# Transformer block on one core: another order inside the attention steps, and four row buffers for the routed tiles

## What is computed

```python
x = x + attention(layernorm(x))          # 16 heads of 32
#   q, k = layernorm(rope(x @ w_q)), layernorm(rope(x @ w_k))   per head
#   a = tril((q @ k.T) ** 4);  out = (a / a.sum(-1)) @ v;  out @ w_out
x = x + moe(layernorm(x))
#   logits = x @ gate.T; scores = sigmoid(logits); 4 of 16 experts chosen, by groups
#   each expert: (silu(x @ g.T) * (x @ u.T)) @ d.T, weighted and added;
#   one shared expert for every token
```

## Time and profile before

| | us |
|---|---|
| three timed runs | 1215.68, 1217.14, 1225.99 (median 1217.14) |
| the profiled execution | 1209.58, its span 1207.6 |
| PE, DVE, ACT, POOL busy | 958.4, 756.9, 563.6, 529.1 |
| the four batches of attention | 118.0, 149.4, 139.7, 112.0 |
| end of attention to the first scatter | 134.5 |
| first to last scatter of the routed tiles | 457.4 |

### The profile page before, as it was taken

How to read it: one execution, slowest core, us unless ns; L and a number is a source line. 1 busy time by engine, 2 the same in 40 slices (tenths; PEclk the granted TensorE clock), 3 DMA queues, 4 the chain that set the end, 5 groups by cost and what they waited for, 6 DMA issues and landing times. The chain is left out here.

```text
span 1207.6 us, 21002 instructions
## 1 busy us (share of the span) xinstructions
PE 958.4 (79%) x5770; PEld 455.7 (38%) x5771; DVE 756.9 (63%) x1663; ACT 563.6 (47%) x1009; POOL 529.1 (44%) x738
## 2 busy tenths in 40 slices
PE   5967789869777785984777799888888798878883
PEld 2432333324333332341343454444344344434441
DVE  2857865867888588849648665554455544545552
ACT  2347874866537665577235234333333233333330
POOL 0005663544415545367302003555555555555553
PEclk9988999888879887976868899899999989999996
DMA  8002333433323333655346896777777777778874
GB/s 330 13 35 93 118 105 137 140 119 112 107 88 100 137 107 110 236 204 192 107 148 207 304 319 184 193 185 184 174 188 191 178 179 181 190 174 193 183 187 78
DMA packets 76648, 193.48 MB, mean 160 GB/s; under 512 B 9904, under 2 KB 11056, under 8 KB 75312
## 3 DMA queue, kind: packets, MB, share of 16 engines
q1 hardware_dynamic: 58672, 149.53, 35.9%
q0 software_dynamic: 17920, 43.26, 19.6%
HBM read 131.67 MB, written 61.10 MB: 160 GB/s over the span
## 5 line engine op out<-in xcount | busy, mean ns | idle before, releaser
L743 PE MATMUL bank<-arena,xgT 128*128 (+1 forms) x1152 | 288.0, 387 | 3.6 <-ACT xgT L1029 3.1
L1065 POOL TENSOR_TENSOR s_p<-s_p,c_causal 128x128 f32<-128x128 f32 x256 | 153.8, 624 | 304.3 <-DVE s_p L1420 282.7
L485 PE MATMUL bank<-arena 128*128 128x512 f32 x384 | 196.5, 663 | 43.8 <-ACT arena L856 14.6
L1022 ACT ACTIVATE hT<-bank 128x512 f16<-128x512 f16 x96 | 57.3, 597 | 273.1 <-PE bank L753 273.1
L743 PEld LDWEIGHTS bank<-arena,xgT 128*128 128x128 f16 x1152 | 109.2, 100 | 133.1 <-issue 45.4
L1073 POOL TENSOR_TENSOR arena<-arena 128x768 f16<-128x768 f32 x68 | 113.0, 1662 | 87.8 <-ACT arena L821 87.7
L1109 POOL DMA_INDIRECT out<-yy,sidx x80 | 128.6, 1608 | 46.1 <-issue 44.6
L764 PE MATMUL bank<-wd,hT 128*128 128x512 f16 x576 | 146.0, 391 | 0.7 <-ACT hT L1022 0.7
L910 ACT ACTIVATE arena<-bank 128x512 f32<-128x512 f32 (+3 forms) x256 | 100.8, 439 | 93.2 <-PE bank L533 92.6
L1694 DVE TENSOR_SCALAR yy<-bank,hsc 128x512 f32<-128x512 f32 x80 | 60.0, 750 | 122.8 <-DMA out<-yy,sidx 116.6
L1029 ACT ACTIVATE xgT<-bank 128x1024 f16<-128x1024 f16 x96 | 98.2, 1023 | 78.7 <-PE bank L734 77.4
(11 more groups left out here) (172 smaller groups left out, 1390.2 us busy)
## 6 DMA issues: line engine op xcount, KB each, us to landing
wd<-w_scratch SPq DMA_DIRECT2D x82, 512.0 KB, 4.2
arena<-w_experts SPq DMA_DIRECT2D x34, 768.0 KB, 6.0
w_scratch<-arena SPq DMA_DIRECT2D x34, 768.0 KB, 4.5
arena<-w_scratch SPq DMA_DIRECT2D x17, 1024.0 KB, 7.7
xin<-x SPq DMA_DIRECT2D x4, 1024.0 KB, 5.5
arena<-x SPq DMA_DIRECT2D x4, 1024.0 KB, 4.8
x_scratch<-arena SPq DMA_DIRECT2D x4, 1024.0 KB, 5.2
xg<-xn_scratch SPq DMA_DIRECT2D x16, 256.0 KB, 4.5
```

The lines of the kernel that those rows point to most:

```text
L485: mm = pe.matmul(bk[:], xnT[:, c, m * P:m * P + P], wqkv[:, c, w * E:w * E + E], start=(c == 0), stop=(c == EC - 1))
L743: mm = pe.matmul(bank[2 + k][:], xgT[:, k, xh * EC + c, :], w, start=(c == 0 and xh + wh == 0), stop=(c == EC - 1 and xh == 1))
L1065: pool.tensor_tensor(d, d, C["causal"][:], ALU.mult).then_inc(p4_masked, 1)
```

## The change

It has two parts.

**In the attention steps** pieces are put in another order. PE runs `values` of a group's last block ahead of the v product instead of behind it, and in the last batch the logits are spread over steps 5 and 6. ACT does both halves of `qkT` ahead of the first square (the second half stood behind the second square), `copy_v` of blocks 1 to 3 moves from the head of step `4 m + 1` to the end of step `4 m`, `head_squares` moves to the end of step `4 m`. Most other entries of ACT's table move from the head of a step to the end of the step before, which is the same place. DVE's `finish` moves from the head of step `4 m + 1` to step `4 m`, right behind its `fourths`, and `choice_places` goes ahead of `centre`; in the last batch some of the routing goes one step later. SP's store of the normed rows goes one weight half earlier.

**In the routed tiles** the gathered rows have four buffers instead of two, POOL issues the gather of tile `t + 2` where it issued that of `t`, gather and scatter numbers have a semaphore each, and the loops of PE and POOL take four tiles in a turn; ACT, DVE and SP keep two.

```diff
 class Tile:
+    def turns(self, bufs, d=0):
+        n = self.n // bufs
+        c = self.lo // bufs + 1 + d
+        return c if self.r is None else (self.r if n == 1 else self.r * n) + c
...
+def tile_pairs(eng, lo, hi, step, n=2):
+    with eng.Fori(0, (hi - lo) // n) as r:
+        for j in range(n):
+            step(Tile(r, lo + j, n))
...
# SP
-                halves_of(b, 0, 2)
+                halves_of(b, 0, 1)
                 if b:
                     sp.wait_ge(xn16_ready, b)
                     sp.dma_start(xn_dram[N * (b - 1):N * b, 0:E]...
-                halves_of(b, 2, 4)
+                halves_of(b, 1, 4)
...
# PE
-                elif i == 5:
-                    for m in range(MB):
+                elif i in (5, 6):
+                    pe.wait_ge(x2T_sb, upto(pb, 3))
+                    for m in (2 * i - 10, 2 * i - 9):
                         logits(pb, m, bkA)
...
                     scores(b, i)
+                    if i and i % MB == 0:
+                        values(b, i - 1)
                     if b + 1 < B:
                         fill(b, i)
-                    if i:
+                    if i % MB:
                         values(b, i - 1)
...
-                    pe.wait_ge(xg_in[k], t.plus(-TB).uses() * 16)
+                    pe.wait_ge(xg_in[k4], t.plus(-TB).turns(4) * 16)
...
# ACT, sequence
                     square(b, i, 1)
-                    if nb < B and p == 0:
-                        if m:
-                            qkT(nb, m - 1, bkA, bkB, (1,))
-                        head_squares(nb, m)
                     square(b, i, 2)
                     fourth(b, i, 1)
                     square(b, i, 3)
                     fourth(b, i, 3)
+                    if nb < B and p == 0:
+                        if m:
+                            copy_v(nb, m, bkA)
+                        head_squares(nb, m)
...
                     split_next(b, i)
+                    if nb < B:
+                        behind(b, i)
...
# DVE
-                if p == 1 and m:
-                    finish(b, m - 1)
-                elif p == 2 and (m < MB - 1 or lb < B):
+                if p == 2 and (m < MB - 1 or lb < B):
...
                 if p == 0:
                     if m:
+                        finish(b, m - 1)
                         split_qk(nb, m - 1)
                     head_variance(nb, m)
...
+                if i == 15 and b:
+                    choice_places(pb, bkA)
+                if p == 3 and (m < MB - 1 or lb < B):
                     centre(nb if m < MB - 1 else lb, (m + 1) % MB)
...
# POOL
             def weight_and_rows(t):
                 weight(t.plus(-2))
                 pool.wait_ge(weights_here, t.at(-1 - TB))
-                pool.wait_ge(numbers, t.at(-1 - TB) * 2 if not t.below(TB + 4) else t.at(2 - TB))
-                if t.is_(NT - 1):
-                    gather_numbers(t.plus(-1), again=True)
-                else:
-                    gather_numbers(t.plus(1))
-                gather(t)
+                if t.r is not None or t.lo < NT - 3:
+                    pool.wait_ge(gather_no, t.at(3 - TB))
+                    gather_numbers(t.plus(3))
+                    gather(t.plus(2))
+                elif t.is_(NT - 3):
+                    pool.wait_ge(gather_no, RT)
+                    gather(t.plus(2))
+
+            def add_rows(t):
+                pool.wait_ge(y_sb, t.at(-3))
+                if not t.below(TB + 5):
+                    pool.wait_ge(added, t.at(-4 - TB) * 16)
+                pool.wait_ge(scatter_no, t.at(-3 - TB))
+                scatter_numbers(t.plus(-3))
+                scatter(t.plus(-4))
```

159 lines of the change are left out of this document (75 added, 84 removed).

## The result

The changed kernel takes 1228.59 us (median of 15 runs, 1219.36 to 1246.18) against 1217.14 us of the kernel before. The ratio is 1.008, with an interval of 1.005 to 1.011; a second measurement gave 1.012 (1.008 to 1.016). The ratio leaves out the slow runs, four of the 15 that were over 1.5% above the fastest; the median of the other eleven is 1226.7 us. So the kernel is slower by about 1%, and the forecast of 1192 us had the wrong sign. The time lies inside the stated range of 1160 to 1240, in the part that belongs to the first rival.

What follows compares the result with a forecast made beforehand. The prediction took the routed stage as a chain of scatters and attention as bound by badly timed meetings of in-order streams. Gains of 20 us in attention and 5 in routed tiles gave 1217.1 - 25 = 1192 us, range 1160 to 1240.

Steps and rivals of the forecast that it cites:

- the first rival: Routed tiles: earlier weight load gets ahead of the scatter; 40 tiles cost 44 us, giving 1236, up to 1280; chance 0.2.
- More than some 0.8 us: Routed tiles: a down-weight load issued further than this behind a scatter does not delay the next scatter.
- the interval settles there: Routed tiles, first rival: once loads delay scatters, the long interval persists; 40 tiles cost 44 us, all 79 cost 87.
- The 7 us from tiles in which gather and load push each other into the scatter: Routed tiles: these collisions go, the mean interval of 5.79 us falling to the ordinary 5.7, gaining 7 us.
- what is late next is DVE: Attention, stall before `copy_v`: DVE limits the early store's gain to 5 of 7.9 and 3.5 of 5.9 us.
- I expect little: Attention, `finish` ahead of the choice: of 33.5 us waits, gains 2, 2.5 and 1 us in batches two to four.
- I cost it at nothing: Attention, ACT's new order of `qkT` and `head_squares`: no loss expected, at most 11 us over three batches.
- the attention gain is swallowed: Attention: PE's removed stalls return as waits for `fourths`; 0 to 10 us remain, 1205 to 1217; chance 0.17.
- the gather set the pace: Routed tiles: the interval falls towards 5.38 us, 32 us less, 1165, down to 1150; chance 0.1.
- instruction fetches: Routed loops: longer bodies stall on fetching, 20 turns costing 38 us, giving 1230; chance 0.03.
- The share-by-packets variant of the first: Routed tiles: load and scatter share DMA engines packet by packet, about half the loss, some 20 us for 40 tiles.
- rows of several: Routed tiles, sign of being wrong: scatter intervals of 6.5 us and more, several in a row.

Runs made afterwards that it cites:

- the pinned kernel: Changed kernel with the down-weight load also waiting for POOL's weight copy, and that copy for PE's `down`; ratio to the kernel before 0.964, again 0.960.
- the one with the old distance of gathers: Changed kernel with four row buffers and loops in fours kept, but each gather issued for tile t as before; ratio to the kernel before 0.970.
- the kernel of the load at the scatter: New attention order with old routed tiles, but the down-weight load waits until DVE has written yy of the tile two before; ratio to the kernel before 1.073.
- the attention part alone: Kernel before with only the attention reordering, routed tiles as before; 1167.3 us beside 1209.9, ratio 0.967.
- with `finish` back: New attention order on the kernel before, old routed tiles, DVE's `finish` put back behind the choice of experts; ratio to the kernel before 0.978.
- with `copy_v` back: New attention order on the kernel before, old routed tiles, `copy_v` and `head_squares` put back at their old places; ratio to the kernel before 0.992.
- the loops of four: Kernel before with only PE's and POOL's loops over routed tiles taking four tiles in a turn; ratio 1.001.

## Why the prediction was wrong, point by point

**The bound was read rightly.** "A chain of scatters", with PE's wait for rows as slack: the pinned kernel and the one with the old distance of gathers have nearly the same interval, 5.69 and 5.91 us, though PE waits for rows only in the second.

**The step that failed is the border in the first rival.** The prediction saw the mechanism and its place: with PE free, the load of the down weights comes 2.6 us earlier and falls some 1.2 us behind a scatter. That was right to a tenth: by the medians the load comes 9.48 - 6.81 = 2.7 us earlier, and at the ordinary interval this is 6.81 - 5.7 = 1.1 us behind the next scatter. What was wrong is that this distance is harmless. "More than some 0.8 us" rested on a single row, a load 0.3 us behind a scatter that cost 1.1 us; no row said where the cost ends. The curve shows that 0.5 to 1.0 us is the worst place of all, that at 1.0 to 1.4 the interval is still 6.2 us in the median without the kernel of the load at the scatter, and that nothing is lost only from 1.5 on. So by its own estimate of the place, good to half a us as it said, the forecast stood on the wrong side, and the case that it called likeliest could not last: in the tiles from 1013.08 on one load at 1.29 us makes an interval of 6.17, which puts the next load at 0.64 us, and that interval is 7.40. In place of the 5 us that the routed tiles were to gain, the stretch between first and last scatter became 65 us longer.

**How it settles.** The prediction said that "the interval settles there, since a later scatter doesn't move the load". The runs show the point: the load falls 6.81 us less the interval behind the scatter, and the table has intervals of 6.6 to 6.8 us at distances about zero; both hold at 6.6 to 6.8. The intervals swing around it: a long one puts the load earlier, and the next is shorter. The priced loss of 1.1 us for an interval was high (0.83 measured), and "40 tiles, 44 us" low in tiles: 63 intervals over 6.3 us, 65 us in all. The first rival's 1236 us came within 8 us with two errors that cancel: the loss was 21 us larger than its 44, and attention gained 20 to 25 us more than forecast.

**The routed terms.** The additional waiting instruction (2 us lost) doesn't show: the pinned kernel has it and the shortest interval. The 7 us from tiles in which gather and load push each other into the scatter came only with the load held behind: the interval is then 5.58 to 5.69 us.

**The attention terms were too small by half.** 20 us forecast, 40 by the timed runs. One wrong step is the discount "what is late next is DVE", therefore 5 of 7.9 and 3.5 of 5.9 us. Undoing the store cost 7.7 and 6.8: the stall was worth its full length. "I expect little" of `finish` was wrong as well, 5.5 us against 15, but not by the argument that `fourths` still stand behind the choice. Where that was made, in the third batch, undoing cost 3.3 us and the forecast was 2.5; PE's wait for `finish` in that batch is 12.2 us with `finish` back; with it ahead it is 1.6 us, and 4.5 us more go to POOL's mask. What was missed are the first batch, to which it gave nothing (4.2 us), and the second (6.4 against 2). The two rows of that wait in the third batch, with `finish` back and in the attention part alone:

```profile
PE bank L548 <- DVE arena L1367: 12.2, 2, 11.2
...
PE bank L548 <- DVE arena L1367: 1.6, 1, 1.6
```

Nor did its list of stalls have PE's waits for `qkT`, 6.3 us in the first batch before. "I cost it at nothing" for `qkT` was right (1.6 us). The first batch, 4 us forecast, gained 9.7, and 4.2 are lost again when `finish` goes back; with `copy_v` back the batch is longer than before the change, which no wait row of before could show.

**The rivals.** The second (the attention gain is swallowed) is refuted by the attention part alone. The third (the gather set the pace) too: POOL's landing wait grew, and even with the load pinned the early gathers reach 5.69 and 5.58 us, not the 5.38 of a chain without traffic. The fourth (instruction fetches) by the loops of four, 1.001. The share-by-packets variant of the first, half the loss, didn't come out: at the distance of its row, 0 to 0.5 us, the interval is 6.81 against 5.67 us, the whole 1.1 us.

**What was to show it.** Four of the signs came: no wait for rows, PE waiting for `h`, no store ahead of `copy_v`, and in the third batch a wait for POOL's mask in place of the one for `finish`. Batches two and three were shorter by more than forecast, 16 and 11 us. POOL's landing wait did not stay at 80 us, and with it came "rows of several" with intervals over 6.5 us, which the prediction named as the sign of being wrong.

## What to carry to other kernels

When a wait disappears, follow what the freed engine triggers until you reach a shared resource, and ask at which time relative to the critical transfer it arrives. If the answer rests on a border, measure the border before betting on a side: one row gives a point and no border. A transfer on the critical chain can be protected by an explicit order (here a load that waits for something just behind the scatter's issue, a ratio of 0.96 instead of 1.01), since otherwise its neighbours move with changes elsewhere; and such a hold must have nothing urgent queued behind it (1.20 and 1.22 with the gather there).

A reordering of streams that meet often is one thing, not a list of edits: take it apart by undoing, and don't expect the parts to sum to the whole.

## What was unexpected

- An indirect scatter's packets start 2.18 us after its issue, while SP's load has its own mostly 1.3 to 2.0 us after, and 0.9 in one kernel. So a load issued up to 1.4 us *behind* a scatter can be ahead of it at the DMA engines. At 0.5 to 1.0 us behind, 512 KB lengthen the interval by 1.7 us and 256 KB by 0.4.
- The loss has its maximum next to the point where it ends: 7.4 us at 0.5 to 1.4 us behind where the load's first packet comes in time, 5.7 from 1.5 on.
- A chain whose disturber is tied to the link before can find a slow balance: 6.6 us against the 5.7 that the same instructions reach when two waits are moved.
- The granted clock, a mean over a stretch of its full level (2.4 GHz) and half of it, was 0.85 in the second batch before, where PE had stood still for 5 to 8 us three times, and 0.95 in the attention part alone, where the longest stall is 4.2 us. That batch became 17.4 us shorter, and PE's busy time in it fell from 117.0 to 111.9 us for the same work. The two don't always go together: in the third batch a stall of 11.0 us went, and the clock was 0.87 before and 0.88 in the attention part alone.
